# An equivariant graph layer on 412,500 edges: the receiver's half of the first product from a table per node, and the pieces of the hidden values subtracted in PSUM

## The reference: what is computed

```
xs, xd = x[src], x[dst]
s1 = [xs scalars (8), xd scalars (8)];  v1 = [xs vectors (8x3), xd vectors (8x3)]
h  = relu(emb @ fc1_w1 / sqrt(10));  w = h @ fc1_w2 / 4        # 16 hidden values, then 512 weights
Wss, Wvv, Wsv, Wvs = w in four blocks of 16x8
s_t = a1 * (s1 . Wss + (v1 . r) . Wvv)                          # 8 scalars
v_t = a1 * ((s1 . Wsv) outer sqrt(3) r + v1 . Wvs)              # 8 vectors
second layer: the same shape with 384 weights from fc2, in blocks of 8x8 (Ass, Avv, Bss, Bvv, Csv, Cvs)
edge_out = [tanh(scal), vecs * tanh(gates)] * edge_weight
out = layernorm(x + segment_sum(edge_out, dst))
```

## Time and profile before

| | us |
|---|---|
| runs, median of 3 (lowest to highest) | 6061.76 (6061.47 to 6062.57) |
| span of the profiled execution | 6434.2 |
| TensorE busy (products), of that span | 5895.3 |
| VectorE busy | 5884.2 |
| GpSimd busy | 4974.7 |
| ScalarE busy | 3993.5 |

### The profile page before, as it was taken

How to read it: one execution, slowest core, us unless ns; L and a number is a source line. 1 busy time by engine, 2 the same in 40 slices (tenths; PEclk the granted TensorE clock), 3 DMA queues, 4 the chain that set the end, 5 groups by cost and what they waited for, 6 DMA issues and landing times. The chain is left out here.

```text
span 6434.2 us, 221220 instructions
## 1 busy us (share of the span) xinstructions
PE 5895.3 (92%) x68616; PEld 5688.0 (88%) x68616; DVE 5884.2 (91%) x7326; ACT 3993.5 (62%) x12507; POOL 4974.7 (77%) x6875
## 2 busy tenths in 40 slices
PE   4999999999999999999999999999999999999997
PEld 3898989889999988988999889889989899999997
DVE  7899999999999998989999989999999899999998
ACT  5666666666666666666666666666666566666663
POOL 6777777777778777877877778777878778787884
PEclk9999999999999999999999999999999999999998
DMA  5444444444444444444444444444444444444442
GB/s 144 89 87 85 88 91 87 86 88 89 87 88 91 86 88 88 89 86 85 92 87 87 87 85 91 86 86 88 92 86 92 85 86 93 86 93 87 92 88 54
DMA packets 1671119, 569.93 MB, mean 89 GB/s; under 512 B 1535146, under 2 KB 1619083, under 8 KB 1670536
## 3 DMA queue, kind: packets, MB, share of 16 engines
q1 hardware_dynamic: 1567911, 516.43, 36.8%
q0 software_dynamic: 103168, 53.03, 6.0%
HBM read 302.19 MB, written 7.26 MB: 48 GB/s over the span
## 5 line engine op out<-in xcount | busy, mean ns | idle before, releaser
L1043 PE MATMUL p<-identity,prods 128*128 128x128 f32 x29016 | 3580.0, 276 | 157.1 <-issue 81.0
L654 POOL DMA_INDIRECT nodes<-x_rows,idx x3224 | 3104.0, 963 | 704.7 <-issue 615.1
L1043 PEld LDWEIGHTS p<-identity,prods 128*128 128x128 f32 x29016 | 3219.4, 143 | 185.0 <-issue 163.6
L1038 PE MATMUL pw<-w_stack,hid_t 128*128 128x128 bf16 x22568 | 1679.3, 220 | 229.6 <-issue 110.8
L1038 PEld LDWEIGHTS pw<-w_stack,hid_t 128*128 128x128 bf16 x22568 | 1435.3, 99 | 316.6 <-issue 138.9
L1292 DVE TENSOR_TENSOR prods<-pw,V 128x2048 f32<-128x2048 f32 x403 | 922.6, 2289 | 177.2 <-remote 83.3
L1337 DVE TENSOR_TENSOR prods<-pw,M 128x1024 f32<-128x1024 f32 x806 | 975.9, 1211 | 15.9 <-issue 6.7
L1347 DVE TENSOR_TENSOR prods<-pw,VT 128x1536 f32<-128x1536 f32 x403 | 704.8, 1749 | 59.7 <-remote 53.2
L870 ACT ACTIVATE off_hot<-node_iota,off_base 128x42 f32<-128x42 f32 x3216 | 747.1, 318 | 0.0
L1314 DVE TENSOR_TENSOR prods<-pw,S 128x1024 f32<-128x1024 f32 x403 | 490.0, 1216 | 84.6 <-PE pw L1038 76.0
L610 POOL TENSOR_TENSOR vr<-V,r 128x384 f32<-128x384 f32 x403 | 347.5, 862 | 244.9 <-issue 185.5
(11 more groups left out here) (136 smaller groups left out, 8242.5 us busy)
## 6 DMA issues: line engine op xcount, KB each, us to landing
dstb<-in_dst SPq DMA_DIRECT2D x403, 504.0 KB
nodes<-x_rows,idx POOLq DMA_INDIRECT x3224
emb_stack<-emb_parts SPq DMA_DIRECT2D x2418, 20.0 KB
emb<-in_emb_t SPq DMA_DIRECT2D x403, 40.0 KB
hid_t<-hid_parts SPq DMA_TRANSPOSE x806
idx<-in_src SPq DMA_DIRECT2D x403, 4.0 KB
xw<-x SPq DMA_DIRECT2D x403, 7.9 KB
vecs<-in_vec SPq DMA_DIRECT2D x403, 12.0 KB
```

The lines of the kernel that those rows point to most:

```text
L654: nc.gpsimd.indirect_dma_start(nodes[:, p, t, side, :], None, x_rows, bass.IndirectOffsetOnAxis(ap=idx[:, p, side, t:t + 1], axis=0)).then ...
L1038: mm = nc.tensor.matmul(pw[:, slot, t, :], hid_t[:, layer, a.par, t, :], w2_stack[:, lo:lo + W], start=True, stop=True)
L1043: return nc.tensor.matmul(out, column, identity[:, :], start=first, stop=last, is_transpose=True)
```

## The change

1. The first layer's weights are made for the sender's half only: 256 in place of 512, five kinds in place of seven. Its products on VectorE have half the elements, and V and S hold senders only. The rows `xw`, the copies `dstb` and the one-hots behind them are gone.
2. For the receiver's half there is a table in DRAM, `t_rows`: for each node and each of the 16 hidden values 64 numbers, the node's values times the receiver's half of fc1_w2. TensorE makes it in chunks of 64 nodes from bf16 pieces of x, four chunks ahead of its use and one chunk every two periods (`nodes_made`, `store_nodes`).
3. Edges are now laid out in tiles of 128 successive ones. A tile's receivers lie within eight nodes (`NEAR`) of its first. `hidden_near` makes the hidden values once more for all eight nodes, with a large negative number (`FAR`) added where the edge is not that node's, so that the relu leaves zero there. `load_near` reads each tile's first receiver into a register and loads the eight nodes' part of the table, 128 rows of 64. `receivers` multiplies both: eight f32 products of 128x64, which start the sums of this half in PSUM; the sender's sums are added to them there.
4. The later pieces of the hidden values are made by subtracting the first ones in PSUM with a matmul by minus the identity (`hidden_less`), and ScalarE rounds what is left (`hidden_second`, `hidden_third`). GpSimd's two subtractions go.
5. Directions, edge weights, sender indices and offsets of the receivers are prepared before the first period, in seven passes over the edges, and stay in SBUF (`r_all`, `w_all`) or are written to DRAM as records (`rec`, `off_rows_of`, `base_rows`). The loads of vectors, inverse lengths and weights leave the period; `stack_off`, `load_near_bases`, `load_near` and `store_nodes` come in.
6. The general path is also taken if a tile spans more than eight nodes.

The core of the diff:

```diff
-            def load_early(a, is_general):
-                ...
-                first = nc.sync.value_load(base_i[0:1, bass.ds(s, 1)], min_val=0, max_val=N - 1)
-                ...
-                sp.dma_start(dstb[:, p, :], every.broadcast_to([ROWS, SUPER])).then_inc(dstb_in[p], 16)
-                wait(sp, xd_mm, two.n(1, 1))
-                sp.dma_start(xw[:, p, :], x3_rows[bass.ds(first * 3, ROWS), :]).then_inc(xw_in[p], 16)
+            def load_near_bases(a):
+                p = a.par
+                sp.dma_start(near_base[:, p, :], base_rows[:, bass.ds(a.index() * G, G)]).then_inc(near_base_in[p], 16)
+            def load_near(a):
+                p = a.par
+                sp.wait_ge(near_base_in[p], a.k(16))
+                ...
+                wait(sp, d_mm, a.before(2).n(1, 1))
+                ...
+                wait(sp, t_stored, a.before(1).k(16, 16 * (LEAD - 1)))
+                ...
+                for t in range(G):
+                    first = nc.sync.value_load(near_base[0:1, p, t:t + 1], min_val=0, max_val=N - 1)
+                    sp.dma_start(t_near[:, p, t, :], t_rows[bass.ds(first * H, NEAR * H), :]).then_inc(t_near_in[p], 16)
+            def stack_off(a):
+                ...
+                sp.dma_start(emb_stack[64:64 + NEAR, p, :].rearrange("j (c e) -> j c e", c=G),
+                             off_rows_of[bass.ds(a.index() * G, G), :, :].rearrange("c j e -> j c e")).then_inc(off_in[p], 16)
+            def store_nodes(a):
+                sp.wait_ge(t_out, a.n(1, 1 + 2 * LEAD))
+                sp.sem_inc(begun, 1)
+                sp.dma_start(t_nodes[bass.ds((a.half + LEAD) * CHUNK, CHUNK), :],
+                             t_stage[0:CHUNK, :, :, :, :].rearrange("n h a j w -> n (h a j w)")).then_inc(t_stored, 16)
+                sp.wait_ge(t_mm, a.n(1, 1 + 2 * LEAD))
+                sp.sem_inc(begun, 1)
+                sp.dma_start(xt[:, 0, :, :], x6[:, :, bass.ds((a.half + (LEAD + 1)) * CHUNK, CHUNK)]).then_inc(xt_in[0], 16)
```

SyncE's period:

```diff
                     if four_on is not None:
                         load_emb(four_on)
                     if three_on is not None:
-                        load_early(three_on, is_general)
-                    zero, one, two, three = (stage(at, by, i) for by in (2, 1, 0, -1))
+                        load_indices(three_on, is_general)
+                    if three is not None and not is_general:
+                        load_late_base(three)
+                    if one is not None and not is_general:
+                        load_near(one)
+                    if three_on is not None and not is_general:
+                        load_near_bases(three_on)
                     if one is not None and i != -1:
                         turn_hid(one, 0)
-                    if zero is not None:
-                        load_vectors(zero)
-                        if i is None or i >= 0:
-                            load_inverse(zero)
                     if two is not None:
-                        load_destinations(two, is_general)
-                    if three is not None:
-                        load_weights(three)
-                    ...
+                        load_late(two, is_general)
                     if three_on is not None:
-                        stack_emb(three_on)
+                        stack_emb(three_on, is_general)
+                        if not is_general:
+                            stack_off(three_on)
                     if one is not None and i != -1:
                         turn_hid(one, 1)
+                    if two is not None and not is_general and two.par == 1:
+                        store_nodes(two)
```

TensorE:

```diff
-            def dst_rows_made(a):
-                ...
-                for t in range(G):
-                    mm = nc.tensor.matmul(xd_ps[:, t, :], hot_t[:, p, t:SUPER:G], xw[:, p, :], start=True, stop=True)
+            def hidden_less(a, piece, made):
+                pe.wait_ge(made, a.n(1, 1))
+                slot = (0, 3)[piece]
+                nc.tensor.matmul(hid_ps, minus_bf[:, :], hid_parts[:, a.par, :, slot * H:slot * H + H], start=False,
+                                 stop=True, skip_group_check=True).then_inc(hid_less, 1)
+            def hidden_near(a, half):
+                ...
+                nc.tensor.matmul(near_ps, w1_near[:, :, :].rearrange("k n h -> k (n h)"),
+                                 emb_stack[:, p, 512 * half:512 * half + 512], start=True, stop=True).then_inc(near_mm, 1)
+            def receivers(a, before, is_general):
+                ...
+                    pe.wait_ge(near_out, a.n(2, 2))
+                    pe.wait_ge(t_near_in[a.par], a.k(16 * G))
+                for t in range(G):
+                    ...
+                        mm = nc.tensor.matmul(z[:, :, t, :], hid_near[:, P * t:P * t + P],
+                                              t_near[:, a.par, t, :].rearrange("p (c w) -> p c w", w=C), start=(t == 0), stop=(t == G - 1))
-            columns = (384, 0, 256, 128, L1, L1 + 128, L1 + 256)
+            columns = (0, 128, 256, 384, 512)
             def scalar_sums(a):
-                for u in range(2 * C):
-                    mm = added(st_t_ps, prod_s[:, u, :, :, :].rearrange("p a t w -> p (a t w)"), u == 0, u == 2 * C - 1)
+                for u in range(C):
+                    added(st_t_ps, prod_s[:, u, :, :, :].rearrange("p a t w -> p (a t w)"), u == 0, False)
+                for h in range(2):
+                    mm = added(st_t_ps, dots[:, 2 * h:2 * h + 2, :, :].rearrange("p a t w -> p (a t w)"), False, h == 1)
```

VectorE's products (the third, scalar, cross and dot products go from 1024 to 512 elements in the same way):

```diff
-                    wts.unsqueeze(1).broadcast_to([P, 2, G, 2 * C, C]),
-                    V[:, p, 0:2, :, :].unsqueeze(4).broadcast_to([P, 2, G, 2 * C, C]), ALU.mult).then_inc(pv_done, 1)
+                    weights(0, ring, 0).unsqueeze(1).broadcast_to([P, 2, G, C, C]),
+                    V[:, p, 0:2, :, :].unsqueeze(4).broadcast_to([P, 2, G, C, C]), ALU.mult).then_inc(pv_done, 1)
+            def receiver_dots(a):
+                ...
+                nc.vector.tensor_tensor(dots[:, 0:3, :, :], z[:, 5:8, :, :], r_of(a), ALU.mult).then_inc(dvv_done, 1)
+            def vectors_made(a):
+                ...
+                nc.vector.tensor_tensor(VT[:, a.par, :, :, :], vs, svr[:, :, :, :], ALU.add).then_inc(vt_done, 1)
```

More of the change, by code:

```diff
@@ new lines, in load_late_base, with load_rows @@
+            def load_late_base(a):
+                p = a.par
+                wait(sp, acc_done, a.before(2).n(1, 1))
+                sp.sem_inc(begun, 1)
+                sp.dma_start(late_base[:, p, :], base_rows[:, bass.ds(a.index() * G, G)]).then_inc(late_base_in[p], 16)
+            def load_rows(c):
+                h = c % 2
+                for (landed, pieces) in zip((dst_in, src_in, wgt_in, vec_in), row_loads[c]):
+                    for to, of in pieces:
+                        sp.dma_start(to, of).then_inc(landed[h], 16)
@@ L713, in body @@
                     if zero is not None:
-                        gathers(zero, 0, (7,))
-                    if zero is not None and is_general:
-                        pool.sem_inc(gathers_begun, 1)
-                        gathers(zero, 1, range(G))
+                        gathers(zero, (7,))
                 periods(pool, body)
@@ L998, in _, with turn @@
         def _(pe):
-            pe.wait_ge(s_const, 11)
-            pe.wait_ge(s_excess, 1)
-            for c in range(SCAN):
-                mm = nc.tensor.matmul(p1[0:1, P * c:P * c + P], span[:, 2, c:c + 1], identity[:, :], start=True, stop=True)
-            mm.then_inc(s_bases, 1)
+            def turn(c, q, of, ready, value):
+                nb = blocks_of(c)
+                pe.wait_ge(ready, value)
+                wait_kept(pe, c - 1, q)
+                for b in range(nb):
+                    n = tiles_of(BLOCKS * c + b)
+                    mm = nc.tensor.transpose(turned_banks[q][:, P * b:P * b + n], of[0:n, b, :], identity[0:n, 0:n])
+                mm.then_inc(turned, 1)
@@ L1168, in body @@
-                    if one is not None and not is_general:
-                        dst_rows_made(one)
                     if four is not None:
                         four_sums_turned(four, windows, more)
+                    if zero is not None:
+                        hidden_less(zero, 0, hid_a)
+                    if three is not None:
+                        if two is not None:
+                            pe.wait_ge(pss_done, two.n(1, 1))
+                        else:
+                            pe.wait_ge(pgf_done, three.n())
+                        fill(three, 2, at.par)
@@ new lines, in _ @@
+            last = recs[:, NS - 1 - (NCH - 1) * BLOCKS * P // G, G:2 * G].bitcast(F32)
+            wait_kept(dve, NCH - 1, 1)
+            if NS != FULL:
+                done(nc.vector.scalar_tensor_tensor(last, last, 1.0, fresh[:, :], ALU.subtract, ALU.mult))
```

(20 more changed lines are left out.)

1420 lines of the change are left out of this document (849 added, 571 removed).

## The result

The changed kernel takes 9648.97 us (median of 4 runs, 9646.24 to 9651.29), the kernel before 6061.61 on the same chip (4 runs, 6059.76 to 6062.57): 1.5915 times, 95% interval 1.5892 to 1.5937. The prediction was 9200 us, range 6850 to 10400: the direction and the place were right, and the time is 449 us (4.9%) above the predicted one.

What follows compares the result with a forecast made beforehand. SyncE's in-order queue, nearly full beside VectorE and TensorE, was to become the period: start 184 + 403 x 23.6 + tail 70 = 9765 us, times 0.942 = 9200 us. Range 6850 to 10400; the forecast's own 7810 to 10620.

Steps and rivals of the forecast that it cites:

- The bound: SyncE's in-order issue queue, nearly full before, becomes the period at 23.6 us; VectorE has 11.3 us of work, TensorE 13.5.
- The sum of the queue: SyncE's issues per period: 10.8 us kept plus 12.8 us added make 23.6 us, between 20.2 and 27.1.
- The pair: One value load (0.77 us) and its DMA (0.53) in `load_near`: 1.30 us, 1.03 to 1.62; eight are 10.4 us.
- The start: Row passes in seven chunks before the first period replace the scan, adding 100 us to 84 (0 to 200).
- the ratio 0.942: Whole time: the summed profiled span of 9765 us is scaled by 0.942, as the profiled execution was 6.1% longer than the median.
- The waits of SyncE: SyncE's waits for other engines cost nothing, covered by 23.6 minus 13.5 us; uncovered, some 2 to 3 us a period.
- The engines' work: Per period, VectorE falls to 11.3 us and TensorE to 13.5; both are busy 50 to 60%, and TensorE's clock may fall.
- The wait for t_near that was named: Sign in the profile after: VectorE and TensorE wait for t_near, the transposes and the stacks.
- (1): SyncE's issue steps are mostly not spent outside a profile; TensorE sets 14.1 us a period, 5590 us; chance 0.15.
- (2): SyncE's value loads cost little at a fixed address, only issues count: 17.4 us a period, 6850 us; chance 0.09.
- (3): SyncE's waits are not covered, adding a chain of 3 us: 26.6 us a period, 10340 us; chance 0.05.
- (4): The program takes its general path, every period going through 298 windows: 13 ms; chance 0.01.

Runs made afterwards that it cites:

- the run with one load: Changed kernel with one value load instead of eight, all eight DMAs taking their address from the first tile: 7853.85 us.
- rebalanced: Changed kernel with one load of eight registers for the bases and both transposes of the hidden values issued by ScalarE: 6875.45 us.
- one pair: Changed kernel with one value load and one DMA filling all eight parts of t_near from the first tile's rows: 6852.63 us.

## Why the prediction was right, and where its sizes were off

**The bound.** Right: SyncE's in-order queue was nearly full before and is the period after, with no wait of its own. Shown from both sides: 32 more transposes on TensorE cost nothing, and less on SyncE gave the time back until its waits began.

**The sum of the queue.** Predicted 10.8 kept and 12.8 added; measured, from the timeline above: near loads from the end of the late_base issue, 5012.10, to the near_base issue, 5021.98, 9.88 us (10.4 predicted), near_base 0.65 (0.5), stack_off 0.58 (0.7), and `store_nodes` in every second period (5009.90 - 5007.30) - (5032.10 - 5031.90) = 2.4 us, 1.2 a period (0.7, and 0.5 for waits and increments). Together 12.3, which leaves 23.17 - 12.3 = 10.9 for what was kept. The pair is 1.12 to 1.14 us and not 1.30: its DMA is the 0.53 that was read from the neighbouring issue; the value load was taken at 0.77 from rows of a TENSOR_LOAD of 0.451 us, and here the load is 0.269 us and the whole step 0.6 (0.64 by the run with one load). It lay inside its bounds of 1.03 to 1.62.

**The start.** The first of VectorE's vector products starts at 272.9 us, where it was 83.8 before, and the last one 67.8 us ahead of the end:

```profile
L1689 DVE TENSOR_TENSOR prods<-pw,V x403: 1200/1225/1226, 272.9 to 9581.0; 128x1024 f32<-128x1024 f32 x135
```

So the new start costs 189 us where 100 were taken, near the upper end of the 0 to 200; how it divides among the passes over the edges and the first chunks of the table was not taken apart. In the prediction's count, with 403 periods where 402 lie between these two starts, start and tail come to 311 us and not 254, 57 more. Some of the difference between 89 and 57 is that one period too many.

**The step that made the 449 us: the ratio 0.942.** The sum before it was 9765 us; periods too long by 0.43 x 403 = 173 us and the start and tail too short by 57 bring it to 9649. The factor took 565 us off. It assumed that a profiled execution is 6.1% longer than a timed run whatever the kernel. The kernel before is (6434.2 against 6061.8), the changed one is not (9648.8 against 9648.97), nor are the experiments with a shorter period (6874.5 against 6875.45 rebalanced; 6845.2 against 6852.63 with one pair). The changed kernel's profile is one of its four timed runs (9650.94), while that of the kernel before is none of its own: its timed runs beside the experiments list spans of 6058 to 6068 us at a granted clock of 0.995 to 0.996, its profile 6434.2 us at 0.983. What lengthened that one execution is open; no run here takes it apart. The factor was the one term without a mechanism behind it.

**The waits of SyncE, costed at nothing.** Right in the changed kernel, for the reason given: the queue was the slowest. The cover was overrated, though. The text put it at 23.6 - 13.5 us of TensorE work, but the period need only fall to 19.04 us for the first waits to show (1.0 us in 5000), and at 16.2 they are 0.9 us a period; with ScalarE's passes delayed by 4 us they were there at 22 us. As these waits read, what matters is the loop from the stacks through ScalarE's hidden passes, `hidden_near` and back to `stack_emb`, and not TensorE's busy time.

**The engines' work.** VectorE 3983.76/345.2 = 11.5 us a period (11.3 predicted) and the granted clock fell from 0.99 to 0.83, as said. TensorE's busy time is 16.1 us at that clock, 68% of the span, above the 50 to 60% that were named. In the rebalanced kernel, at clock 0.94, it is 4419.97 us in 5000, 14.4 us in a period of 16.29, where 13.5 was predicted and 14.6 stands for before at 0.99: the busy time hardly falls, though part of what is missing is the lower clock. The wait for t_near that was named has no row from 1000 to 9000 us; the transposes' has.

**The rivals.** (1) Issue steps that shrink outside a profile: refuted, the timed runs have the profile's length, and dropping seven issues gave 0.36 to 0.48 us each in timed runs. By that rule of the Trainium skill ("DMA: Bandwidth & Descriptors", Anatomy of one DMA: 50 ns of dispatch) eight issues would be 0.4 us; the rows have 8 x 0.53. The prediction's estimate of 0.43 us from the Trainium skill's 512 cycles an instruction is nearer; in the page "DMA: Bandwidth & Descriptors" that figure stands under "Why a DMA increments its semaphore by 16 and not by 1", not in the section that the prediction names. Even with the queue relieved, this rival's 5590 us, TensorE at 14.1 us a period, wasn't reached. (2) Cheap value loads: refuted, a load and its steps cost 0.64 us; with seven of the eight gone the period is 18.7 us, where the rival's 17.4 and one load of 0.77 make 18.2. (3) Uncovered waits of 3 us: not in the changed kernel; a wait of that size, 3.4 us, shows only with half the pairs on ScalarE. (4) The general path was not taken.

**The subtraction in PSUM.** The prediction had "GpSimd loses two subtractions" and TensorE 0.22 us more, no effect. Right for this kernel and incomplete as an account: the subtraction also moves the last hidden piece earlier, past GpSimd's gathers, and TensorE waits 4.6 us a period less. That is 1581 us where SyncE doesn't hide it, with GpSimd's order as it is here. So the change holds a part whose queue time costs more than the rest saves, and one that is worth nothing until the first is repaired.

**What stays open.** No version here beats the kernel before. To match it with the new start, a period would have to be (6062 - 311)/403 = 14.3 us. The best that computes everything, 16.29 us, has SyncE waiting 0.4 us and TensorE busy 14.4; how much of the remaining 2.0 us the stop of 1.1 us for ScalarE's hidden pass makes was not measured by itself, as the one edit that removed it put a longer wait in its place.

## What to carry to other kernels

Before adding small DMAs with computed addresses, put the issuing engine's queue on the timeline and sum it per period like an engine's work: the page has no busy row for it, and eight pairs of value load and DMA (9 us) cost more here than the 3 us of VectorE's work that they saved. Load several addresses with one instruction, and when issues are moved to another engine, place them behind what the slowest loop needs from that engine. An edit that measures as nothing under one bound has not been measured: look for the wait that it makes or removes, and price that wait for the day the cover goes.

## What the runs showed of the hardware

- A register load from SBUF on SyncE is 0.269 us for one value and 0.720 us for eight in one instruction; alone, with range check and address steps, one costs 0.60 to 0.64 us of the queue in this loop.
- An issue's length differs with its form, and not by the number of its rows: 0.338 us for 128 rows of t_rows, 0.48 for the same 128 rows eight times in one DMA, 0.32 for off_rows_of (eight rows in eight pieces), 0.76 for an emb_stack issue (ten rows in eight pieces), with (4.94 - 0.76)/5 = 0.84 from one to the next.
- With SyncE's queue full, 32 more transposes on TensorE moved the time by 0.08% and two subtractions more on GpSimd by 0.01%.
- Two engines that issue DMAs at the same time didn't lengthen each other's issues: pairs of load and DMA were 1.11 us apart on SyncE and 1.05 on ScalarE.
- TensorE's granted clock was higher in the runs in which it idled less: 0.83 with 16.1 us of work in 23.17 us, 0.90 with 18.7 us, 0.94 at a period of 16.3 us. But the busy share doesn't fix it: with half of the pairs behind `hidden_second` it was 0.83 at a share of 78%, with one load of eight registers 0.88 at 79%. The same 128x128 f32 transpose has a mean of 326 ns in the changed kernel and 294 ns with the added ones, over windows that mix the two levels of 1.2 and 2.4 GHz.
